# Key tiles of 128 keys, packed scatters, experts and combination moved forward, and expert pairs in a software pipeline behind the attention

## The chip, the cores and the metric

The kernel runs on one core of one Trainium2 chip. The metric is the device time of one execution in microseconds (us), of which lower is better; three executions of the kernel before are shown, and their median counts. Engines are named as in the profile: PE is TensorE's multiplication, PEld its weight load, DVE VectorE, ACT ScalarE, POOL GpSimd and SP SyncE, which only issues transfers.

## The reference

Eight images of 64 channels and 56 x 56 pixels pass through three stages, in float32:

```python
x = x + conv3x3(group_norm(x, 32 groups), weight)        # 64 -> 64 channels
t = tokens(x)                                            # 3136 tokens of 64 per image
t = t + softmax(q(ln(t)) k(ln(t))^T / 8) v(ln(t))        # one head of 64, each image by itself
n = ln(t)
logits = n @ gate_w + gate_b                             # 16 experts
top-2 of softmax(logits), renormalised -> dispatch
h = silu(n @ w1[e]) * (n @ w2[e])                        # hidden 128
t = t + sum_e dispatch[e] * (h @ w3[e])
```

## The kernel before, in words

An image's 3136 tokens are cut in 7 chunks of 448 tokens (CHUNK, CHUNKS), a chunk in 4 tiles of 112 (TILE, PER), an image so in 28 tiles (TILES). There are 56 chunks (ALL). The program is one list of **bodies**, written out in full, one for each chunk: body n = 7u + c attends with the 448 queries of chunk c of image u. Bodies -8 to -1 come ahead of the attention, bodies 0 to 55 attend, and bodies 56 to 77 come behind it. A body is a row of 28 slots, i = 0 to 27, and in each slot every engine's program has at most one step of each kind, in the same order on all. Nothing reorders them: an engine that waits holds back all of its later steps, of later bodies too.

Slot i of a body that attends, on PE: `scores` (L1047, L1049) multiplies key tile i with the body's queries, in two fp32r parts q_a and q_b, into one of two banks ps_s; ACT takes its exponential (L636) into one of 6 tiles prob; every fourth slot `weigh` (L1060) multiplies four such tiles with the values v_s into ps_o, in plain float32, the even tiles in the upper and the odd ones in the lower half of the array's columns. Between them stand the **maxima for the next body**: 28 products of a query tile with 448 keys (L1026), each reduced to its row maximum on DVE (L788), spread over slots 2 to 24 by `max_reach` (MAX_FROM, MAX_TO). They give the shift of the next body's exponentials (`shift`, L1034, slot 26).

STEPS lists the other work and its slot; LAG says how many bodies a stage runs behind (or ahead of) the attention. *pre* (7 bodies ahead): convolution, tokens, first layer norm, keys k_a and values v_s of the next image. *post* (1 behind): attended tokens into `kept`, second layer norm, gate, top 2; in the body of chunk 0, slots 14 to 26 also **route** the image that has just ended: counts, ranks and places (`slot`) of all its tokens among the experts. *scatter* (8 behind, one chunk a body): POOL copies each token's row twice into sorted_x in HBM, with 8 indirect transfers of 112 rows (L502). *experts* (15 behind): per chunk of sorted rows 5 **pairs** of 128-row tiles, 2 in the last chunk, 32 an image. A pair is four steps on PE, each followed by one on ACT or DVE: `fx` transposes, `hidden` multiplies with w1 and w2 (fp32r, two parts), ACT's tanh and DVE's two products, `turn` transposes, `down` multiplies with w3 and ACT copies into fy, which SP stores to sorted_y. *combine* (22 behind): POOL gathers with 8 indirect transfers (L515), waiting for the whole image's fy (L509) and for the combination before it (L510, the buffers got1, got2 and tc are single); DVE weighs and adds (L944 to L949) in slot 19, PE transposes, ACT copies, SP stores the output.

So the 22 bodies behind the attention are: 56 with the last post and route; 57 to 63 with the scatter of image 7; 56 to 70 with 66 pairs (EXPERT_STEPS_ALONE, four slots a pair); 56 to 77 with a combination each. POOL's order in a body is scatter, norm2, norm1, gather (`body`, L527). Ahead of the first image POOL sets constants (L442 to L477) and zeroes both sorted_x with 28 transfers (L483); its first step of the group norm (L535) is behind them.

## Time and profile before

| | us |
|---|---|
| three executions, median (lowest to highest) | 3304.51 (3299.92 to 3306.05) |
| the profiled execution: its own time | 3304.37 |
| its span | 3301.5 |
| ahead of the first score / bodies 0 to 55 / behind the last score | 198.8 / 2701.4 / 401.3 |

| engine | busy us | share of the span |
|---|---|---|
| PE | 2755.8 | 83% |
| DVE | 1950.5 | 59% |
| ACT | 1426.9 | 43% |
| POOL | 1004.9 | 30% |

The profiled execution is 0.14 us from the median, and 2.9 us of it lie outside of its span. Lines L1047 to L1085 are in PE's functions, L788 to L949 in DVE's, L553 to L636 in ACT's and L502 to L535 in POOL's. Matmul records give the time from a product's start to its end with the array's latency in it, so consecutive ones overlap; from one start to the next is what a product takes of PE.

### The profile page before, as it was taken

What the parts mean: (1) busy time and instruction counts of PE and PEld (TensorE: products, weight loads), DVE (VectorE), ACT (ScalarE), POOL (GpSimd) and SP (SyncE); (2) the same over time, 40 slices, a digit from 0 to 9 for tenths busy, and PEclk for the clock granted to TensorE, in tenths of its full rate; (3) what the DMA queues carried; (4) which work ended last, traced back from release to release, by engine and by line L of the source; (5) the groups of instructions that cost most, each with busy time, mean ns of one, the idle gap of its engine ahead of it and who ended that gap; (6) DMA issues with size and microseconds to landing.
All of it is one profiled execution on the core that took longest, in us unless ns stands there. A gap on an engine that the chain in (4) does not pass through costs nothing.

```text
span 3301.5 us, 47374 instructions
## 1 busy us (share of the span) xinstructions
PE 2755.8 (83%) x14345; PEld 1688.3 (51%) x14345; DVE 1950.5 (59%) x5316; ACT 1426.9 (43%) x3169; POOL 1004.9 (30%) x1084
## 2 busy tenths in 40 slices
PE   0489998998999999998999899998999898967760
PEld 0245554554555555555555455554555555545550
DVE  1366667667666666668566765667656656442221
ACT  0134444444555544554445454454544454523330
POOL 4000002221212134234242332423324323347444
PEclk9679999999999999999999999999999999965555
DMA  6200000111111111211112111111111111123321
GB/s 142 63 21 20 19 16 26 30 29 33 47 43 41 44 44 50 54 44 52 51 50 52 49 49 51 50 49 40 50 47 41 38 43 43 42 64 91 82 60 31
DMA packets 218415, 156.13 MB, mean 47 GB/s; under 512 B 94400, under 2 KB 208832, under 8 KB 218176
## 3 DMA queue, kind: packets, MB, share of 16 engines
q1 hardware_dynamic: 187008, 106.12, 12.2%
q0 software_dynamic: 31168, 46.98, 5.9%
q8 instruction: 131, 2.15, 0.3%
q14 instruction: 108, 0.88, 0.1%
HBM read 89.29 MB, written 63.70 MB: 46 GB/s over the span
## 4 chain that ended last, share of the span: by engine, by line
PE 58%; DVE 24%; issue 8%; POOL 6%; ACT 2%; DMA 2%; SPq 1%; POOLq 0%; DVEq 0%; ACTq 0%
PE ps_o L1060 17%; DVE max_part L788 9%; PE ps_s L1047 8%; PE ps_m L1026 8%; PE ps_s L1049 6%; PE ps_x L1202 5%; PE ps_z L1085 4%; POOL got L515 3%; PE ps_x L1217 2%; PE ps_z L1210 1%; POOL sorted_x L502 1%; PE ps_y L1136 1%; PE ps_y L1120 1%; DVE top_i L845 1%; DVE got L944 1%
## 5 line engine op out<-in xcount | busy, mean ns | idle before, releaser
L788 DVE TENSOR_REDUCE max_part<-ps_m 112x1 f32<-112x448 f32 x1568 | 947.9, 621 | 528.5 <-PE ps_m L1026 518.9
L636 ACT ACTIVATE prob<-ps_s 112x448 f32<-112x448 f32 x1568 | 848.9, 543 | 598.8 <-PE ps_s L1049 575.1
L1026 PE MATMUL ps_m<-k_a,q_a 128*112 128x448 f32 x1568 | 589.3, 394 | 140.4 <-DVE max_part L788 129.5
L1060 PE MATMUL ps_o<-prob,v_s 112*64 112x448 f32 x3136 | 695.9, 566 | 0.3 <-issue 0.3
L1047 PE MATMUL ps_s<-q_a,k_a 128*112 128x448 f32 x1568 | 661.9, 422 | 16.0 <-ACT prob L636 9.9
L1049 PE MATMUL ps_s<-q_b,k_a 128*112 128x448 f32 x1568 | 573.5, 366 | 0.0
L502 POOL DMA_INDIRECT sorted_x<-xn,slot x448 | 427.3, 954 | 283.7 <-issue 260.3
L515 POOL DMA_INDIRECT got<-sorted_y,slot x448 | 424.9, 948 | 213.8 <-issue 126.5
L1026 PEld LDWEIGHTS ps_m<-k_a,q_a 128*112 128x112 f32 x1568 | 276.4, 176 | 311.1 <-DVE max_part L788 273.1
L525 POOL TENSOR_TENSOR ln_s<-ln_s,minus_half 112x4 f32<-112x4 f32 x56 | 58.1, 1037 | 1175.7 <-DVE ln_s L706 1175.7
L1047 PEld LDWEIGHTS ps_s<-q_a,k_a 128*112 128x112 f32 x1568 | 276.2, 176 | 184.5 <-issue 123.4
L1060 PEld LDWEIGHTS ps_o<-prob,v_s 112*64 112x64 f32 x3136 | 193.9, 138 | 310.4 <-issue 283.7
L1049 PEld LDWEIGHTS ps_s<-q_b,k_a 128*112 128x112 f32 x1568 | 277.1, 177 | 12.9 <-issue 3.0
L932 DVE SCALAR_TENSOR_TENSOR up<-th,ps_x 128x256 f32<-128x256 f32 x256 | 107.3, 419 | 271.1 <-ACT th L604 270.9
L1202 PE MATMUL ps_x<-w_hi,fxT 128*128 x512 | 204.5, 402 | 15.1 <-ACT fxT L600 9.4
L521 POOL TENSOR_TENSOR ln_s<-ln_s,minus_half 112x4 f32<-112x4 f32 x56 | 56.4, 1007 | 445.9 <-DVE ln_s L706 445.9
L1085 PE MATMUL ps_z<-xg,wT 128*64 128x224 f32 x1344 | 153.4, 381 | 35.2 <-ACT xg L553 35.2
L609 ACT ACTIVATE hidT<-ps_z 128x256 f32<-128x256 f32 x190 | 73.1, 385 | 233.6 <-PE ps_z L1210 233.6
L604 ACT ACTIVATE th<-ps_x 128x256 f32<-128x256 f32 x256 | 98.5, 385 | 155.7 <-PE ps_x L1202 154.0
L1202 PEld LDWEIGHTS ps_x<-w_hi,fxT 128*128 128x128 f32 x512 | 107.7, 210 | 112.6 <-issue 88.2
L1202 PE MATMUL ps_x<-w_lo,fxT 128*128 x512 | 158.6, 313 | 0.0
L782 DVE TENSOR_TENSOR q_b<-ps_y,q_a 128x448 fp32r<-128x448 f32 x56 | 35.0, 625 | 208.9 <-ACT q_a L624 208.9
(170 smaller groups left out, 3004.0 us busy)
## 6 DMA issues: line engine op xcount, KB each, us to landing
fx<-sorted_x SPq DMA_DIRECT2D x48, 384.0 KB
sorted_y<-fy SPq DMA_DIRECT2D x48, 320.0 KB, 3.1
fx<-sorted_x SPq DMA_DIRECT2D x56, 256.0 KB
xh<-in_x SPq DMA_DIRECT2D x96, 126.0 KB, 2.7
x_st<-in_x SPq DMA_DIRECT2D x100, 112.0 KB, 2.6
sorted_x<-fy POOLq DMA_DIRECT2D x24, 320.0 KB
sorted_x<-xn,slot POOLq DMA_INDIRECT x448
got<-sorted_y,slot POOLq DMA_INDIRECT x448
```

Of the source, the lines that this page charges most:

```text
L502: g.indirect_dma_start(out=sorted_x[b % 2], out_offset=bass.IndirectOffsetOnAxis(ap=slot[:, b % 4, k, j:j + 1], axis=0), in_=xn2[:, j, :, ...
L515: g.indirect_dma_start(out=got[:, j, :], out_offset=None, in_=sorted_y[b % 2], in_offset=bass.IndirectOffsetOnAxis(ap=slot[:, b % 4, m, ti ...
L604: a.activation(th[:], ps_x[:].rearrange("p (t m h) -> p t m h", t=2, m=2)[:, :, 0, :], ACT.Tanh, scale=0.5).then_inc(s["th_ready"], 1)
L636: a.activation(prob[(at.n * TILES + i) % PROBS][:], ps_s[i % 2][0:TILE, 0:CHUNK], ACT.Exp).then_inc(s["p_ready"], 1)
L788: v.tensor_reduce(max_part[:, m % PER, m // PER:m // PER + 1], ps_m[m % 2][0:TILE, 0:CHUNK], AX.X, ALU.max).then_inc(s["max_red"], 1)
L932: v.scalar_tensor_tensor(out=up[:], in0=th[:], scalar=1.0, in1=both[:, :, 0, :], op0=ALU.add, op1=ALU.mult).then_inc(s["f_link"], 1)
L1026: t.matmul(ps_m[m % 2][0:TILE, 0:CHUNK], q_a[:, bass.ds(n % 2, 1), j * TILE:(j + 1) * TILE].rearrange("p a c -> p (a c)"), k_a[u % 2][:, k ...
L1047: t.matmul(ps_s[i % 2][0:TILE, 0:CHUNK], k_a[p][:, keys], q_a[:, now, :].rearrange("p a c -> p (a c)"), start=True, stop=False)
L1049: t.matmul(ps_s[i % 2][0:TILE, 0:CHUNK], k_a[p][:, keys], q_b[:, now, :].rearrange("p a c -> p (a c)"), start=False, stop=True).then_inc(s ...
L1060: t.matmul(ps_o[side:side + CHANNELS, 0:CHUNK], v_s[u % 2][:, i, :], prob[(n * TILES + i) % PROBS][:], start=(i < 2), stop=(i >= TILES - 2 ...
L1085: last = t.matmul(ps_z[64 * half:64 * half + 64, 0:CHUNK // 2], wT[:, down, k, :], xg[:, top:top + ROWS // 2, k:k + SIDE], start=(down == ...
L1202: last = t.matmul(ps_x[:, j * 2 * HIDDEN:(j + 1) * 2 * HIDDEN], fxT[:, j * SLOTS:(j + 1) * SLOTS], w12[part][:, bass.ds(picked[2 * pair + ...
```

## The change

1. **Key tiles of 128.** The image's 3136 keys become 25 tiles (KEY_TILES) of 128 places. Chunks 0 to 5 fill 112 places of tiles 0 to 23; of chunk 6, one tile of 112 tokens goes to tile 24, and the other three (GIVING) are cut in 21 pieces of 16 keys, which fill places 112 to 127 of tiles 0 to 20. Tiles 21 to 24 keep 16 empty places (key 0, value and its weight 0). A body has 25 slots instead of 28: 25 `scores`, exponentials of 128 rows and `weigh` products. The maxima stay 28 products of 448 keys, but the last 4 of a body, and every seventh body's queries, are now two products, of 112 and 336 keys, and all read keys in pieces. The values of the pieces go from v_give to v_s with 7 transfers an image on SP. The maxima are spread over slots 2 to 21. The group `weigh` of the last slots has 5 tiles, the others 4. The constants now also hold zeros for v_s and k_a.
2. **Packed scatter.** The image's 7 scatters run in the first three bodies behind it: chunk 0 in that of chunk 0, then three and three. Two semaphores by turns let a scatter start when the one before the last has landed.
3. **Experts and combination sooner.** Experts run 11 behind instead of 15, fy is double. Images 0 to 5 are combined two chunks a body, in the bodies of chunks 5, 6 and 0 (and one in that of chunk 1) from 19 bodies behind their first chunk on; images 6 and 7 one chunk a body, from body 61 (LATE) to 74, at slot 22. got and tc are double, and POOL issues the gather one body ahead.
4. **Pipeline of pairs.** Behind the attention a slot has `fx` of a pair, `hidden` of the pair before, `down` of the pair three before and `turn` of the one two before; `hidden` has two banks, those of ps_s. A body's store of fy is issued one body later, the last two together, behind the output of that body.

```diff
-LAG = {"pre": -CHUNKS, "post": 1, "scatter": 1 + CHUNKS, "experts": 1 + 2 * CHUNKS, "combine": 1 + 3 * CHUNKS}
+LAG = {"pre": -CHUNKS, "post": 1, "experts": CHUNKS + 4}
+SCATTERS = ((0,), (1, 2, 3), (4, 5, 6), (), (), (), ())
+COMBINES = {5: (0, 1), 6: (2, 3), 7: (4, 5), 8: (6,)}
+COMBINE_AT, COMBINED_AT = (10, 16, 22), (11, 18, 23)
+LATE = ALL + 5
+LAST = LATE + 2 * CHUNKS - 1
 EXPERT_STEPS = sorted(
-    (at + 5 * g, order, name, g) for g in range(PAIRS) for at, order, name in
+    (at + (0, 4, 8, 13, 17)[g], order, name, g) for g in range(PAIRS) for at, order, name in
...
-MAX_FROM, MAX_TO = 2, 25
+MAX_FROM, MAX_TO = 2, 22
-PROBS = 6
-SHIFT = 26
+PROBS = 7
+KEY_TILES = -(-TOKENS // 128)
...
+SHIFT = 23
+    def combines(self):
+        if self.n >= LATE:
+            return [(2, ALL - 2 * CHUNKS + self.n - LATE)] if self.n <= LAST else []
+        image, place = (self.u - 3, self.c + CHUNKS) if self.c < 2 else (self.u - 2, self.c)
+        chunks = COMBINES[place] if place in COMBINES and 0 <= image < BATCHES - 2 else ()
+        return [(slot + 2 - len(chunks), CHUNKS * image + c) for slot, c in enumerate(chunks)]
...
+def expert_steps(at):
...
+    steps, pairs = [], alone_pairs()
+    here = [k for k, (mine, _) in enumerate(pairs) if mine.n == at.n]
+    if here and here[-1] == len(pairs) - 1:
+        here += [len(pairs) + k for k in range(3)]
+    for place, k in enumerate(here):
+        for name, behind in (("fx", 0), ("hidden", 1), ("gated", 1), ("down", 3), ("turn", 2)):
+            if 0 <= k - behind < len(pairs):
+                steps.append((1 + 4 * place, name) + pairs[k - behind])
...
+        def keys_of(p, c):
+            k = key_tiles(p)
+            if c < CHUNKS - 1:
+                return [(0, CHUNK, k[:, c * PER:(c + 1) * PER, 0:TILE])]
+            own = OWN * TILE
+            return [(0, own, k[:, KEY_TILES - OWN:KEY_TILES, 0:TILE]), (own, CHUNK, k[:, 0:FILLED, TILE:128])]
...
+                for mine in at.stores():
...
+                    wait_apart(sp, s["fy_ready"], ONE + mine.pairs_before() + mine.pair_count())
...
             for p in range(2):
-                chain(g.memset(v_s[p][:, :, 0:1], 1.0))
+                chain(g.memset(v_s[p][96:128, :, :], 0.0))
+                chain(g.memset(v_s[p][0:TILE, :, 0:1], 1.0))
+                chain(g.memset(key_tiles(p)[:, FILLED:KEY_TILES, TILE:128].bitcast(f32), 0.0))
+            chain(g.memset(v_give[:, :, 0:1], 1.0))
...
+                early = at.scatters() if at.c else []
+                early = early[:1] if at.attends else early
+                for m in early:
+                    scatter(m)
...
+                for _, k in At(*divmod(at.n + 1, CHUNKS)).combines():
+                    gather(k)
+                for m in at.scatters()[len(early):]:
+                    scatter(m)
...
-                    t.matmul(ps_m[m % 2][0:TILE, 0:CHUNK],
-                             q_a[:, bass.ds(n % 2, 1), j * TILE:(j + 1) * TILE].rearrange("p a c -> p (a c)"),
-                             k_a[u % 2][:, kb * CHUNK:(kb + 1) * CHUNK], start=True, stop=True).then_inc(s["max_done"], 1)
+                    for first, last, keys in keys_of(u % 2, kb):
+                        done = t.matmul(ps_m[m % 2][0:TILE, first:last],
+                                        q_a[:, bass.ds(n % 2, 1), j * TILE:(j + 1) * TILE].rearrange("p a c -> p (a c)"),
+                                        keys, start=True, stop=True)
+                    done.then_inc(s["max_done"], 1)
```

## Rows read from the trace of the kernel before

**Rows 1.** The page: busy time by engine; TensorE's granted clock in 40 slices.
```profile
PE 2755.8 (83%) x14345; PEld 1688.3 (51%) x14345; DVE 1950.5 (59%) x5316; ACT 1426.9 (43%) x3169; POOL 1004.9 (30%) x1084
PEclk9679999999999999999999999999999999965555
```
**Rows 2.** Stages: stretch, length, busy us (instructions) by engine, clock, DMA share, GB/s.
```profile
198.80:2900.20 2701.40, 2474.46 (x13168) 1478.90 (x13169) 1774.36 (x4847) 1304.73 (x2852) 743.78 (x774) 0.99 0.16 41
2900.20:3301.50 401.30, 216.70 (x918) 173.35 (x916) 109.72 (x285) 106.75 (x292) 219.30 (x233) 0.54 0.27 67
```
**Rows 3.** The same view for bodies 3, 17, 25, 26, 28 and 52, in this order.
```profile
317.30:358.30 41.00, 38.25 (x197) 21.57 (x197) 27.48 (x75) 18.44 (x38) 2.01 (x2) 1.00 0.07 18
926.70:975.60 48.90, 45.98 (x259) 28.56 (x258) 31.36 (x85) 25.39 (x58) 9.64 (x10) 1.00 0.17 45
1327.30:1377.90 50.60, 46.64 (x262) 28.89 (x261) 32.73 (x89) 25.70 (x59) 17.23 (x18) 1.00 0.20 53
1377.90:1430.20 52.30, 48.24 (x261) 29.33 (x260) 32.72 (x89) 25.58 (x59) 17.31 (x18) 0.97 0.20 51
1481.70:1534.90 53.20, 45.91 (x230) 25.71 (x229) 42.29 (x113) 22.76 (x49) 21.92 (x23) 0.97 0.25 64
2713.30:2761.50 48.20, 43.36 (x231) 26.75 (x230) 29.05 (x78) 24.30 (x56) 16.19 (x17) 1.00 0.17 43
```
**Rows 4.** Timeline of PE in body 3: start us, length us, engine, line, operation.
```profile
344.92 0.36 PE L1026 MATMUL ps_m<-k_a,q_a 128*112 128x448 f32 x1
345.12 0.36 PE L1047 MATMUL ps_s<-q_a,k_a 128*112 128x448 f32 x1
...
345.83 1.72 PE L1060 MATMUL ps_o<-prob,v_s 112*64 112x448 f32 x8
347.48 0.45 PE L1047 MATMUL ps_s<-q_a,k_a 128*112 128x448 f32 x1
```
**Rows 5.** Timeline of PE's weight loads in the same stretch.
```profile
344.92 0.17 PEld L1047 LDWEIGHTS ps_s<-q_a,k_a 128*112 128x112 f32 x1
```
**Rows 6.** PE's longest wait in bodies 17, 25, 28 and 52: us, times, longest.
```profile
PE ps_m L1026 <- DVE max_part L788: 1.8, 2, 1.1
...
PE ps_m L1026 <- DVE max_part L788: 2.9, 3, 1.1
...
PE ps_m L1026 <- DVE max_part L788: 4.0, 3, 2.9
...
PE ps_m L1026 <- DVE max_part L788: 3.5, 4, 1.0
```
**Rows 7.** Timeline of PE: four value tiles in body 26.
```profile
1419.10 3.08 PE L1060 MATMUL ps_o<-prob,v_s 112*64 112x448 f32 x8
```
**Rows 8.** Timeline of POOL ahead of the first image.
```profile
17.93 0.64 POOL L476 MEMSET fy<- 128x640 f32 x1
...
72.73 0.58 POOL L535 TENSOR_TENSOR gn_rstd<-gn_var,minus_half 128x1 f32<-128x1 f32 x1 [1.75 <-DMA sorted_x<-fy]
```
**Rows 9.** Timeline of POOL behind the attention: scatters and gathers, idle time in brackets.
```profile
2931.35 1.07 POOL L502 DMA_INDIRECT sorted_x<-xn,slot  x1 [11.84 <-issue]
...
2941.47 0.95 POOL L515 DMA_INDIRECT got<-sorted_y,slot  x1 [0.30 <-issue]
...
3200.56 0.93 POOL L515 DMA_INDIRECT got<-sorted_y,slot  x1 [8.57 <-DMA sorted_y<-fy]
...
3209.21 0.94 POOL L515 DMA_INDIRECT got<-sorted_y,slot  x1 [0.30 <-issue]
```
**Rows 10.** Busy time in one body of five pairs behind the attention; columns as in rows 2.
```profile
3098.10:3116.20 18.10, 15.47 (x66) 12.92 (x65) 5.73 (x14) 7.68 (x21) 7.84 (x10) 0.50 0.34 82
```
**Rows 11.** Timeline of SP: the last store of fy.
```profile
3197.52 0.48 SPq L415 DMA_DIRECT2D sorted_y<-fy  x1
```
**Rows 12.** Timeline of all engines at the end.
```profile
3290.46 0.93 POOL L515 DMA_INDIRECT got<-sorted_y,slot  x1 [0.30 <-issue]
3292.84 0.76 DVE L944 TENSOR_TENSOR got<-got,gates 112x256 f32<-112x256 f32 x2 [11.87 <-DMA got<-sorted_y,slot]
```

More of the change, by code:

```diff
@@ L430, in _ @@
+            for n in range(-CHUNKS - 1, LAST + 1):
+                at, nxt = [At(*divmod(m, CHUNKS)) for m in (n, n + 1)]
+                body(at, (nxt.u + 1, nxt.c) if n >= -CHUNKS and nxt.u + 1 < BATCHES else None)
             sp.wait_ge(s["stored"], ONE + 16 * ALL)
@@ L499, in scatter @@
                     wait_apart(pool, s["fx_b_in"], ONE + (b - 1) * (CHUNKS - 1) * 16)
-                for j in range(at.chunk("scatter") * PER, (at.chunk("scatter") + 1) * PER):
+                for j in range(c * PER, (c + 1) * PER):
                     for k in range(TOP):
@@ L1239, in body @@
                 done = 0
-                for i in range(TILES):
+                experts = expert_steps(at)
+                for i in range(KEY_TILES):
                     if at.attends:
```

363 lines of the change are left out of this document (201 added, 162 removed).

## The prediction

> **What bounds the kernel now.** I read the page first, then the stages, then single bodies, then the timelines. PE is busy 83% of the span, and the clock row falls only ahead of the attention and behind it [rows 1]. The attention is 2701.4 us with PE busy 2474.5 of them; behind it lie 401.3 us in which PE is busy 216.7 and POOL 219.3 [rows 2]. The two stages have different limits.
>
> In the attention PE sets the pace. A light body (no experts) takes 41.0 us with PE busy 38.3; with five pairs 48.9 and 46.0; with a combination too 50.6 and 46.6 [rows 3]. So a pair costs (48.9 - 41.0) / 5 = 1.58 us and a combination 1.7. What PE does not fill is nearly all one wait, that of the maxima's bank for DVE: 1.8 us, 2.9 with a combination, 4.0 in a body that routes [rows 6]. DVE itself is busy only 31 to 33 us of these, 42 in the routing one [rows 3]: it is late at single moments, when layer norms or combinations stand ahead of a reduction, not as a whole.
>
> Behind the attention nothing is full for long; it is a row of serial stretches: 31.1 us of last post and route up to the first scatter (2900.2 to 2931.35), seven bodies in which POOL does 8 scatters and 8 gathers, the experts of image 7 at some 18.1 us a body [rows 10], and from 3200.56 the gathers of image 7, each waiting for the combination before it [rows 9].
>
> **Key tiles of 128.** Three slots go from each of 56 bodies. By starts, a score product takes 0.20 us (344.92 to 345.12 for its like), and four value tiles 1.65 (345.83 to 347.48), 0.41 each [rows 4]: 3 x (0.20 + 0.20 + 0.41) = 2.4 us at least. The first product behind other work starts the next 0.08 us later still, so I take 2.6, and 2.8 as the most. ACT loses three exponentials a body, and is not what anyone waits for.
>
> Added: the last four maxima are two products each, with one more weight load. No row has a product of 112 fp32r columns. Its bounds: in proportion the columns are the same and it costs nothing but a start, 0.05 us; or 112 columns take as long as the 448 of the nearest row, 0.20 to 0.25. I take 0.1, near the lower, since the work is the same in columns: 0.4 us a body, 0.2 to 1.0. That keys are read in pieces has no row; I take nothing, the same bounds covering it.
> In the rows the load of 0.17 us lies beside the product before it, as the 0.20 us from start to start leave no room for it [rows 4, 5]. The Trainium skill says otherwise ("TensorE: Matmul & The Clock Gate", Part 3, on the mechanism of tiling): a load overlaps products in flight only if it goes to other rows of the array. By that the four extra loads would stand bare, 0.7 us a body instead of 0.4, 17 us more in the sum. The trace disagrees with it for long products.
>
> That is 2.6 - 0.4 = 2.2 us of PE work less. How much of it becomes time? DVE's work does not shrink, and its 28 reductions now have to fit in slots 2 to 21. Body 52 shows it: it lacks the convolution and first norm, PE is busy 3.3 us less than in body 25, but the body is only 2.4 us shorter, and the wait for DVE 0.6 longer [rows 3, 6]. A quarter of what PE saves goes to the wait. So 2.2 x 0.75 = 1.65 us a body, 92 us in all. Ends: 2.8 - 0.2 with no loss, 146 us; 2.4 - 1.0 with half lost, 39 us.
>
> **Moved into the attention.** Experts 11 behind instead of 15: bodies 11 to 55 hold 207 pairs where bodies 15 to 55 held 190: 17 x 1.58 = +27 us. Combinations: 39 instead of 34, 5 x 1.7 = +9. The routing body had the light chunk of 2 pairs and one combination; now it has 5 pairs and two. DVE's 42.3 us there become 42.3 + 3 x 0.8 + 1.7 = 46.4 (four combining steps of 0.42 [rows 12], and (5.7 - 1.7) / 5, about 0.8, for a pair [rows 10]); its wait was already 4.0 against 2.9 elsewhere. For six such bodies I add 1.3 us each, +8 (0 to 15). POOL's scatters come two or three to a body, some 20 to 30 us of its 48; the norms' powers stand behind one scatter as before. SP gets the waits of two outputs; the next slice is loaded ahead of the second. The 7 transfers of v_give wait for slot 12 on SP, ahead of the load of the next slice, whose own wait is for a later or equal slot; nothing is late by them. Both at nothing; if the slice came late, a body would lose one pair's 1.6 us.
> Attention: -92 + 27 + 9 + 8 = **-48 us** (-110 to +12).
>
> **Ahead of it.** POOL's constants stand before the zeroing, and that before the group norm's power at 72.73, which waits for the last of these transfers [rows 8]. 640 columns take 0.64 us, so the two fills of 1600 take 3.2, and the four small ones about 0.6: **+4 us** (2 to 6).
>
> **Behind the attention.** Times from the last score.
> Post and route: 31 us, plus 3 more pairs' DVE work (2.4) and one more combination (1.7) in body 56, and 2 for waits: 37. 56 scatters without gathers between: 8 take 2931.35 to 2941.47, so 1.25 each [rows 9], 70 us: 107. Landing and the load of the slice, together 5 (1.5 for a gather from 3291.4 to 3292.84 [rows 12], and for the load as much as from the last store to the gather behind it, 3 [rows 9, 11]): image 7's experts start at 112. The 17 pairs of image 6 are hidden under the scatters.
> A pair takes p. Before, five pairs and one combination took 18.1 us, PE 15.5, ACT 7.7, DVE 5.7, all at half clock [rows 10]. The pipeline takes the latencies out: PE's own work then bounds p at (15.5 - 1.0) / 5 = 2.9 at 1.2 GHz, and 1.6, the attention's price, at 2.4 GHz; ACT's part is 1.5. Whether the clock rises no row tells: PE's gaps shrink, yet with a rise they would come back. I take the middle, 2.3.
> Body 60 has 5 pairs, and SP issues the store of image 6's last chunk only behind both loads of body 60, which follow its transposes: 112 + 11.5 = 123.5, plus 3 (store 3197.52 to gather 3200.56 [rows 9, 11]) = 126.5. POOL is idle for those 20 us. First combination at 126.5 + 9.9 + 4.6 (landing, DVE's four steps, transposes and copy) = 141. Each body then ends with a combination, which costs 2.9 on top of its pairs (18.1 = 5 x 3.0 + 2.9): 14.4 us a body, over gathers' 9.9, so the five bodies 62 to 66 end at 213. The last store stands behind that output: 216. Then 56 gathers without waits at 1.236 (3200.56 to 3209.21 for seven [rows 9]), 69, and from the last gather's end to the span's end 10 (3291.4 to 3301.5 [rows 12]): **295 us instead of 401, -106**. At p = 1.6: 274 (-127); at p = 2.9: 313 (-88).
>
> **The sum.** 3304.4 + 4 - 48 - 106 = 3154 us. The profiled run is 0.14 us off the median, so it needs no correction.
>
> **The rivals.**
> (a) *PE's saving is all time.* DVE's waits are of a burst, not a share: 1.0 to 1.1 us is the longest one whatever PE has to do. Then the tiles give 2.4 x 56 = 134, and the time is 3154 - 42 = 3112. Against it: body 52.
> (b) *DVE takes PE's place in the attention.* The reductions lose two slots and the bodies of chunks 5, 6 and 0 get two combinations, each of which lengthens the wait by 1.1 us [rows 6]. Then the tiles give nothing: 3304.4 + 4 + 44 - 106 = 3246. Against it: DVE is busy 65% of a body.
> (c) *The pipeline does not do what it says*: the clock stays at 1.2 GHz, PE is the bound behind the attention, 2.9 a pair: 3172.
> (d) *Slower than before*: the clock falls within the attention. Four value tiles took 3.08 us instead of 1.72 in body 26, behind a wait for DVE, and this body took 52.3 instead of 50.6 [rows 3, 4, 7]; one such fall costs 1.7 us. If each body's denser waits bring them, the loss grows by 1.7 a fall; it turns the sum from 3154 past 3304 at 90 falls, 1.6 a body. With three a body 3154 + 56 x 5.1 = 3440. For it: the waits for DVE grow just there. Against it: bodies of more waits, as 28, show one fall at most.
>
> **How the numbers follow.** The forecast, both gains with a part lost, 0.45; (a) 0.2; (b) 0.12; (c) 0.18; (d) 0.05. The range takes (a), (b) less its far end, (c), and the ends of the tail's p: 3080 to 3230. A measurement of this kernel can tell about 0.2% from no change. All cases but (d) are faster by far more: faster 0.94, same 0.01, slower 0.05.
>
> **What would show it.** Light bodies at 39 us and those with five pairs at 47.3; PE's wait for L788's successor at 2.5 to 4 us a body; a routing body of 57 to 59. Behind the attention: scatters back to back for 70 us, POOL idle 20 us, gathers of image 6 at a body's pace, those of image 7 back to back for 69; a period of 2.3 us a pair between tanhs, and the clock row. A first score later by 4 us. I am wrong if the wait for DVE exceeds 5 us a body, if the split products cost over 0.25 us each, if a wait of SP or POOL that I passed over holds the slices back, or if the clock falls in many bodies.

## The result, and the profile after

The changed kernel takes 3265.0 us in the median (3262.5 to 3266.0) against 3304.3 (3299.9 to 3306.1): 0.9878 of before, with an interval of 0.9867 to 0.989. The forecast was 3154, range 3080 to 3230. So the kernel is faster, as said, but by 39 us and not by 150, and the time lies outside the range.

The page of the changed kernel: PE's busy time, and the granted clock in 40 slices.
```profile
PE 2639.2 (81%) x13913; PEld 1706.6 (52%) x13913; DVE 1953.0 (60%) x5340; ACT 1316.9 (40%) x3009; POOL 1004.7 (31%) x1089
PEclk9679998999999999999899989999999999998785
```
Beside rows 1, PE is busy 117 us less, yet its share has fallen from 83% to 81%, and a few slices of the attention are no longer a 9. The stages of the changed kernel, attention and behind it (columns as in rows 2):
```profile
203.90:2969.00 2765.10, 2446.64 (x12954) 1570.44 (x12955) 1798.45 (x4922) 1232.81 (x2764) 791.85 (x830) 0.96 0.16 43
2969.00:3263.80 294.80, 127.08 (x696) 99.36 (x694) 87.74 (x231) 68.53 (x219) 167.33 (x177) 0.68 0.28 69
```
Ahead of the first score it takes 203.9 us instead of 198.8 (forecast 4 more, got 5). The attention takes 2765.1 instead of 2701.4: the forecast had 48 less, it is 64 more. Behind the last score it takes 294.8 instead of 401.3, where 295 was forecast. The whole miss, 111 us, lies in the attention. Its bodies 2 and 3 (light), 12 (five pairs), 26 (five pairs, two combinations) and 28 (the routing body):
```profile
279.90:321.60 41.70, 37.95 (x190) 22.00 (x190) 27.46 (x75) 16.61 (x36) 2.02 (x2) 0.96 0.07 18
320.00:360.10 40.10, 36.32 (x189) 21.66 (x189) 27.44 (x75) 16.57 (x35) 2.02 (x2) 1.00 0.07 19
713.50:763.20 49.70, 44.50 (x252) 29.33 (x251) 31.24 (x85) 23.47 (x55) 2.01 (x2) 1.00 0.13 35
1426.70:1480.80 54.10, 47.75 (x260) 31.85 (x259) 34.13 (x93) 24.48 (x57) 17.04 (x18) 0.94 0.20 49
1536.00:1598.30 62.30, 52.52 (x262) 35.22 (x260) 45.62 (x120) 25.44 (x58) 12.65 (x13) 0.86 0.16 41
```
Against rows 3, PE does 1.9 us less in light body 3 and 1.5 less with five pairs. Body 3 is only 0.9 shorter, and the one with five pairs is 0.8 longer. Body 2 has the same work as body 3, but the clock falls in it (0.96), and it takes 41.7 us where the light bodies of before take 41.0; bodies 4 and 9 are like it. In bodies 26 and 28 the clock is 0.94 and 0.86. PE's waits in body 12, and one more of body 26:
```profile
PE ps_x L1300 <- ACT fy L686: 2.3, 3, 0.8
PE ps_z L1285 <- ACT hidT L680: 1.7, 3, 0.6
PE ps_m L1119 <- DVE max_part L873: 0.9, 1, 0.9
...
PE ps_y L1243 <- DVE logit L922: 1.8, 1, 1.8
```
The first two are new: in the bodies of before the wait for the maxima was the longest [rows 6], 1.8 us in the one of five pairs, and no wait for ACT reached it. Both come from the offsets 0, 4, 8, 13, 17 of a body's pairs. A pair's turn is in its slot 5, and where the next pair starts 4 slots later that is the next pair's slot 1, its fx, and both write ps_z. Its down is in slot 7, the next pair's 3, its hidden, and both write ps_x. So PE writes a bank, and at once needs it empty. The timeline of PE in body 12:
```profile
726.88 0.44 PE L1308 MATMUL ps_z<-ident,hid 128*128 128x128 f32 x2
727.88 0.41 PE L1285 MATMUL ps_z<-ident,fx 128*128 128x128 f32 x2 [0.56 <-ACT hidT L680]
...
731.47 0.38 PE L1300 MATMUL ps_x<-w_hi,fxT 128*128 x1 [0.75 <-ACT fy L686]
```
Three such pairs of collisions a body make 4 us, where five pairs follow each other in 17 slots instead of 20.

**The ledger of the attention.** To compare kernels I split the attention of each one's profiled execution in three. The waits are the sum of PE's idle times before its products. The half clock is what the clock took: half of the time in which PE was busy at a granted clock of 0.5. The work is the rest: busy time less that half. The three add up to the attention by construction. The half is a rough price: spread 2 has the same products as the changed kernel and comes out with 27 us less work, so its half clock is put too high by about as much.

| kernel | attention | work | waits | half clock |
|---|---|---|---|---|
| before | 2701.4 | 2443.5 | 226.9 | 31.1 |
| changed (first run) | 2765.1 | 2354.3 | 318.5 | 92.4 |
| changed (third run) | 2765.6 | 2353.9 | 317.9 | 93.8 |
| changed, 28 tiles | 2716.2 | 2449.6 | 223.3 | 43.4 |
| early down | 2710.8 | 2349.9 | 314.0 | 47.2 |
| spread 2 | 2732.9 | 2327.5 | 277.4 | 128.1 |
| early down, later combinations | 2723.7 | 2357.5 | 327.2 | 39.3 |
| filler | 2745.4 | 2375.4 | 317.2 | 52.8 |
| one maximum | 2756.1 | 2346.4 | 325.9 | 83.9 |
| early down and filler | 2713.7 | 2363.8 | 304.4 | 45.9 |

From before to after: work 89 less, waits 92 more, half clock 61 more, in all 64 more.

**Behind the attention.** POOL's timeline in the changed kernel: the last scatter of image 7, the first gather behind the idle time, a gather of image 6's last bodies, the first of image 7 and the last of all.
```profile
3073.41 0.94 POOL L561 DMA_INDIRECT sorted_x<-xn,slot  x1 [0.30 <-issue]
3094.50 0.95 POOL L576 DMA_INDIRECT got<-sorted_y,slot  x1 [20.15 <-DMA sorted_y<-fy]
...
3168.23 0.93 POOL L576 DMA_INDIRECT got<-sorted_y,slot  x1 [5.35 <-DVE t_out L1035]
...
3183.91 1.05 POOL L576 DMA_INDIRECT got<-sorted_y,slot  x1 [6.04 <-DMA sorted_y<-fy]
...
3252.80 0.93 POOL L576 DMA_INDIRECT got<-sorted_y,slot  x1 [0.30 <-issue]
```
Nearly all of it stands where the sum had it; the numbers are compared point by point below.

### The profile page after: what moved, and what is told of

Its sections match the earlier page's. It is cut to its first block, busy times and chain, and to the rows that moved or that the text cites. A ratio compares the mean times of both kernels' runs of the same rounds, so it can differ in the third digit from the quotient of the medians.

```text
span 3263.8 us, 46526 instructions
## 1 busy us (share of the span) xinstructions
PE 2639.2 (81%) x13913; PEld 1706.6 (52%) x13913; DVE 1953.0 (60%) x5340; ACT 1316.9 (40%) x3009; POOL 1004.7 (31%) x1089
## 4 chain that ended last, share of the span: by engine, by line
PE 60%; DVE 18%; issue 9%; POOL 6%; ACT 5%; DMA 2%; SPq 1%; POOLq 0%; DVEq 0%; ACTq 0%
PE ps_o L1156 16%; PE ps_m L1119 9%; DVE max_part L873 7%; PE ps_s L1142 7%; PE ps_s L1144 6%; PE ps_x L1300 5%; PE ps_z L1182 3%; PE ps_z L1285 2%; POOL sorted_x L561 2%; PE ps_x L1315 2%; POOL got L576 2%; ACT hidT L680 1%; PE ps_z L1308 1%; ACT fy L686 1%; DVE up L1017 1%
## 5 line engine op out<-in xcount | busy, mean ns | idle before, releaser
L708 ACT ACTIVATE prob<-ps_s 128x448 f32<-128x448 f32 x1400 | 757.4, 543 | 731.9 <-PE ps_s L1144 719.4
L1119 PE MATMUL ps_m<-k_a,q_a 128*112 128x448 f32 (+2 forms) x1792 | 607.5, 383 | 87.0 <-DVE max_part L873 68.3
L1156 PE MATMUL ps_o<-prob,v_s 128*64 128x448 f32 x2800 | 642.6, 568 | 0.0
L1142 PE MATMUL ps_s<-q_a,k_a 128*128 128x448 f32 x1400 | 598.7, 428 | 4.9 <-ACT q_a L700 3.7
L1144 PE MATMUL ps_s<-q_b,k_a 128*128 128x448 f32 x1400 | 524.4, 375 | 0.0
L1142 PEld LDWEIGHTS ps_s<-q_a,k_a 128*128 128x128 f32 x1400 | 273.2, 195 | 115.4 <-issue 88.8
L1156 PEld LDWEIGHTS ps_o<-prob,v_s 128*64 128x64 f32 x2800 | 183.2, 140 | 286.8 <-issue 247.8
L1144 PEld LDWEIGHTS ps_s<-q_b,k_a 128*128 128x128 f32 x1400 | 274.5, 196 | 9.0 <-issue 2.6
L671 ACT ACTIVATE fxT<-ps_z 128x256 fp32r<-128x256 f32 x256 | 98.3, 384 | 276.9 <-PE ps_z L1285 174.2
L1285 PE MATMUL ps_z<-ident,fx 128*128 128x128 f32 x512 | 109.7, 297 | 121.6 <-ACT hidT L680 76.1
```

The source lines that it names most:

```text
L708: a.activation(prob[(at.n * KEY_TILES + i) % PROBS][:], ps_s[(at.n * KEY_TILES + i) % 2][:, 0:CHUNK], ACT.Exp).then_inc(s["p_ready"], 1)
L1119: done = t.matmul(ps_m[m % 2][0:TILE, first:last], q_a[:, bass.ds(n % 2, 1), j * TILE:(j + 1) * TILE].rearrange("p a c -> p (a c)"), keys, ...
L1142: t.matmul(ps_s[t_of % 2][:, 0:CHUNK], k_a[p][:, keys], q_a[:, now, :].rearrange("p a c -> p (a c)"), start=True, stop=False)
L1144: t.matmul(ps_s[t_of % 2][:, 0:CHUNK], k_a[p][:, keys], q_b[:, now, :].rearrange("p a c -> p (a c)"), start=False, stop=True).then_inc(s[" ...
L1156: t.matmul(ps_o[side:side + CHANNELS, 0:CHUNK], v_s[u % 2][:, i, :], prob[(n * KEY_TILES + i) % PROBS][:], start=(i < 2), stop=(i >= KEY_T ...
L1285: last = t.transpose(ps_z[:, j * SLOTS:(j + 1) * SLOTS], fx[:, 2 * pair + j, :, :].rearrange("p a b -> p (a b)"), ident[:])
```

## The experiments

Two theories of the miss in the attention were put against each other. **Theory one**: the key tiles save PE's work as forecast, and the schedule that came with them gives it back, by collisions and by falls of the clock that follow them; repair the schedule and some 90 us come back. **Theory two** (rival b): what PE saves turns into waits whatever the schedule is, because DVE and ACT have each their own chain through a body. What the clock takes was to be told apart from both. In the expectations theory one is A or just the theory, its part on the clock alone is F, and theory two is B.

**The change without its key tiles (tiles28_c).** It ran on one chip with the changed kernel unedited (same_third), filler_c and onemax_c.
```
-    (at + (0, 4, 8, 13, 17)[g], order, name, g) for g in range(PAIRS) ...
+    (at + 5 * g, order, name, g) for g in range(PAIRS) ...
-MAX_FROM, MAX_TO = 2, 22
+MAX_FROM, MAX_TO = 2, 25
-KEY_TILES = -(-TOKENS // 128)
+KEY_TILES = TILES
-SHIFT = 23
+SHIFT = 26
```
and with it the tiles of 112 keys in scores, exponentials and values, the unsplit maxima, no v_give and no zeroing of the tiles.

> The changed kernel unedited, as the base that the other kernels on this chip are held against. On a chip like the first, every theory: 3262 to 3266 us, 0.987 to 0.988 of before, with some 203 us of half clock inside the attention.

> Everything of the change but the key tiles: 28 tiles of 112 keys, maxima to slot 25, and the experts' offsets five slots apart as before. Theory (the tiles save PE some 120 us, and their offsets 0, 4, 8, 13, 17 give all of it back as collisions of a pair's turn and down with the next pair's fx and hidden, and as falls of the clock): PE's waits inside the attention some 230 us instead of 316, half clock some 70 instead of 203, attention 2735 to 2765, time 3235 to 3265, thus no slower than the changed kernel. Rival (the tiles are worth the 92 us net that was forecast, and something else of the change costs them): the changed kernel without its tiles is some 90 us slower, 3355.

Measured: the changed kernel 3264.5 us, 0.9875 (0.986 to 0.9891) of before; without its key tiles **3210.1**, 0.9709 (0.9696 to 0.9723). The key tiles, which should have brought 92 us in the attention, cost 54 in all, 49 of them there. The ledger says how: from 28 tiles to 25, work 96 less, waits 95 more, half clock 50 more. Ahead of the first score there are 5.6 us more (198.2 and 203.8), the zeroing of the tiles, and behind the last 2.9. One light body (3) and one of five pairs (25) of the kernel with 28 tiles, then the same two of the changed kernel:
```profile
317.90:359.20 41.30, 38.15 (x196) 21.58 (x196) 27.36 (x75) 18.32 (x38) 2.01 (x2) 1.00 0.07 18
1367.70:1416.80 49.10, 46.13 (x257) 28.59 (x257) 31.23 (x85) 25.20 (x57) 17.11 (x18) 1.00 0.13 33
```
```profile
319.90:360.00 40.10, 36.31 (x188) 21.65 (x188) 27.45 (x75) 16.60 (x35) 2.02 (x2) 1.00 0.07 19
1377.80:1427.40 49.60, 44.44 (x248) 29.21 (x248) 31.27 (x85) 23.21 (x54) 17.26 (x18) 1.00 0.13 33
```
DVE's time is the same in both. In the light body PE's 1.8 us less become 1.2 less of time, in the body of pairs 1.7 less become 0.5 more. And body 3 is a light body in which the clock holds. The eight light bodies 1 to 5 and 8 to 10 take 332.3 us together with 28 tiles and 332.1 with 25: what the tiles bring there goes to falls in bodies 2, 4, 8 and 9, where 28 tiles have one, in body 8, and to 2.7 us more of waits in body 8. So even where no pair can collide with another nothing is left. My expectation had the kernel with 28 tiles at 3235 to 3265. Its waits are as expected (223 us for 230) and its time at half clock is longer (94 for 70), so what came out smaller is its work.

**Down a slot sooner (early_down).** No down shares a slot with the next hidden any more, but a turn still shares one with the next fx twice a body (slots 15 and 19) instead of three times. It ran on a second chip, with the changed kernel unedited again (same_again) and the two of the next experiment.
```
-    (at + (0, 4, 8, 13, 17)[g], order, name, g) for g in range(PAIRS) for at, order, name in
-    ((1, 1, "fx"), (3, 3, "hidden"), (3, 4, "gated"), (5, 0, "turn"), (7, 2, "down")))
+    (at + (0, 5, 10, 14, 18)[g], order, name, g) for g in range(PAIRS) for at, order, name in
+    ((1, 1, "fx"), (3, 3, "hidden"), (3, 4, "gated"), (5, 0, "turn"), (6, 2, "down")))
```


> The changed kernel once more, unedited, so that the runs beside it have it on their own chip. Ratio to the kernel before 0.988 if the chip is like the first; on a chip like that of the four runs before, where the kernel before takes 3932, all theories leave it open whether it lies with spread (1.005) or onemax (0.991).

> A pair's down stands one slot sooner, and pairs begin in slots 1, 6, 11, 15 and 19, in bodies that attend. No down shares a slot with a hidden any more; two turns share one with an fx instead of three. Theory A (the shared slots are what PE waits in): the waits of hidden for fy (96.6 us) go and those of fx for hidT fall from 76 to about 50; the wait for the maxima's bank rises from 84 towards 137. Net some 70 us of waits, and fewer falls of the clock: ratio to same_again 0.96 to 0.98. Theory B (maxima and DVE are the bound): 0.995 to 1.0, the wait for the maxima taking all of it.

Measured: unedited 3262.4, 0.9872 (0.9855 to 0.9888); early_down **3212.9**, 0.9706 (0.9684 to 0.9727). To the unedited kernel that is 0.985, between the ranges of the two theories (0.96 to 0.98, and 0.995 to 1.0). The waits did not go the way theory one had it. PE's waits are the same in sum, 314.0 us against 315.5 on that chip; only their names have changed. Its body 25:
```profile
1369.90:1419.50 49.60, 43.99 (x249) 28.57 (x249) 31.14 (x85) 23.76 (x54) 17.02 (x18) 1.00 0.13 33
```
and what PE waits for in it:
```profile
PE ps_m L1119 <- DVE max_part L873: 2.3, 3, 1.3
PE ps_y L1228 <- DVE xn L915: 1.3, 1, 1.3
PE ps_z L1308 <- DVE hid L1021: 0.6, 1, 0.6
PE ps_z L1285 <- ACT hidT L680: 0.6, 1, 0.6
```
49.6 us as with the collisions, and 0.5 more than with 28 tiles, though PE has 2.1 less to do. Take a wait for ACT away, and PE is sooner at the next wait for DVE. Nearly the whole gain over the changed kernel, 52 us in the attention, is the clock: half clock 47.2 instead of 93. And beside the kernel with 28 tiles, whose half clock is 43, it is level: 3212.9 and 3210.1, 0.9706 and 0.9709 of before. So with two of six collisions a body left, the key tiles are still worth nothing.

How far is that theory two? Early_down has 91 us more waits than 28 tiles. Of these 50 end with DVE (243 against 193), as theory two says. The other 42 stand ahead of the fx (L1285), two a body, where turns still share a slot with them; the trace names ACT's copy for 22 of them and nothing for 20. These are the schedule's.

**Other places (spread2, early_later).**
```
-    (at + (0, 4, 8, 13, 17)[g], ...          (spread2)
+    (at + (0, 5, 8, 13, 16)[g], ...
```
```
-COMBINE_AT, COMBINED_AT = (10, 16, 22), (11, 18, 23)          (early_later, on top of early_down)
+COMBINE_AT, COMBINED_AT = (12, 16, 22), (13, 18, 23)
```


> Pairs begin in slots 1, 6, 9, 14 and 17: no step of a pair shares a slot with another pair's, nor an fx with the convolution. Two pairs overlap, so that a down follows the next pair's hidden by one slot and waits for DVE's product, some 0.8 us, twice a body. Theory A: the 173 us of shared-slot waits become some 70, ratio to same_again 0.96 to 0.98, near early_down. Theory B: 0.995 to 1.0.

> early_down and the first of two combinations in slot 12 instead of 10. Theory A2 (DVE combines ahead of the logits, PE waits 1.8 us for them in 16 bodies): 28 us less than early_down, with the falls of the clock of these bodies up to 45 less: ratio to early_down 0.985 to 0.992. Rival (the combining is what costs, wherever it stands): 0.997 to 1.0.

Measured: spread2 3224.4 (0.9739, 0.9716 to 0.9762), early_later 3228.6 (0.9772, 0.9755 to 0.9788). In spread2 no step of a pair shares a slot with another pair's. It has the fewest waits of the kernels with 25 tiles (277), but the most half clock, 128, or some 100 with the 27 us that the ledger seems to have put there from its work. Its longest wait is new: a down stands one slot behind the next pair's hidden, and both write ps_x.
```profile
PE ps_x L1315 <- DVE hid L1021: 101.4, 70, 3.0
```
So spread2 is no schedule without waits on a shared bank either. In nearly every body of five pairs its clock falls, and such a body takes 50 us or more. Body 53, five pairs without a convolution, has no fall: 46.5 us, where 28 tiles take 46.6. Bodies of two pairs do gain: the five from 17 to 45 take 42.2 to 42.8 us in early_down, against 43.1 to 43.6 with 28 tiles. (The profiled execution of spread2 took 3235.0 us, the slowest of four from 3210.5 on.) Early_later moves the combination behind the logits, and the wait for logit goes; one for t_out and more for the maxima stand in its place, 13 us more in all, and 8 more of work, against 8 less of half clock. It takes 1.005 of early_down, where 0.985 to 0.992 was expected: to move a single wait gained nothing.

No kernel here has 25 tiles and pairs that never wait on each other's banks. What is shown is that three schedules of pairs (the changed one, early_down, spread2) leave the key tiles worth nothing or less. That every schedule must is not shown.

**The clock (filler_c).** Why does it fall? The timeline of PE in body 28 of the changed kernel, on the chip of same_third:
```profile
1559.44 0.41 PE L1285 MATMUL ps_z<-ident,fx 128*128 128x128 f32 x2 [0.56 <-ACT hidT L680]
...
1563.64 0.98 PE L1243 MATMUL ps_y<-ident,t_out 112*128 112x112 f32 x4 [1.78 <-DVE logit L922]
1564.42 0.98 PE L1315 MATMUL ps_x<-w3s,hidT 128*128 x4
1566.15 0.57 PE L1300 MATMUL ps_x<-w_hi,fxT 128*128 x1 [0.75 <-ACT fy L686]
```
and two stretches of it, up to the fall of the granted clock and from it:
```profile
1559.00:1563.30 4.30, 2.42 (x16) 1.99 (x16) 3.75 (x9) 1.77 (x4) 1.01 (x1) 1.00 0.32 91
1563.30:1570.10 6.80, 5.71 (x21) 4.58 (x23) 3.96 (x22) 2.29 (x6) 5.02 (x6) 0.50 0.13 34
```
PE has idled 1.9 of 4.3 us, at the end of which the clock goes to 0.5, and for 6.8 us PE works at half speed. The wait for logit comes from the moved combinations (at slot 10 DVE has them ahead of the logits, slot 11 needs both); the kernel with 28 tiles has it too, 30.8 us in all. The experiment fills a part of it with products that nobody reads:
```
+                for _ in range(4 if i == 11 and len(at.combines()) == 2 else 0):
+                    t.matmul(ps_s[t_of % 2][:, 0:CHUNK], k_a[p][:, keys], q_a[:, now, :].rearrange("p a c -> p (a c)"),
+                             start=True, stop=True)
                 t.matmul(ps_s[t_of % 2][:, 0:CHUNK], k_a[p][:, keys], ...
```


> Four score products of no use (their result is overwritten) ahead of slot 11's in the sixteen bodies with two combinations, where PE waits 1.76 us for DVE's logits just ahead of a fall of the clock. Theory (the clock falls where PE has just paused twice): the products take the place of part of that pause, and the falls of these bodies go: half clock 203 down to 120 to 150 us, time 3225 to 3245. Rival one (the falls come from elsewhere): half clock still about 200, and the products lie in a wait that was there anyway, 3262 to 3268. Rival two (the products cost their own time and nothing else changes): 16 times 0.9 us, 3277.

Measured: 3247.7, 0.9838 (0.9824 to 0.9852), so 17 us less by adding 68 products; the bodies with two combinations that attend are seventeen. The expected gain was 20 to 40 us. The same body:
```profile
1550.44 0.41 PE L1288 MATMUL ps_z<-ident,fx 128*128 128x128 f32 x2 [0.56 <-ACT hidT L680]
...
1552.01 1.05 PE L1143 MATMUL ps_s<-q_a,k_a 128*128 128x448 f32 x4
...
1554.73 0.57 PE L1246 MATMUL ps_y<-ident,t_out 112*128 112x112 f32 x4 [1.05 <-DVE logit L922]
```
```profile
1550.10:1554.40 4.30, 3.23 (x20) 2.73 (x20) 3.75 (x9) 1.67 (x4) 1.01 (x1) 1.00 0.31 91
1554.40:1561.20 6.80, 4.89 (x27) 3.09 (x27) 4.90 (x25) 2.27 (x6) 5.13 (x6) 1.00 0.16 34
```
PE idles 1.1 us instead of 1.9, and the clock stays. The time at 0.5 in the attention falls from 206 to 111 us, and in the twenty bodies of chunks 5, 6 and 0 from body 12 on, among which are the seventeen of two combinations, from 147 to 65. In the ledger: half clock 41 less, work 21 more, waits 1 less. The wait for logit by itself is not enough for a fall. In early_down it is still 1.58 us in body 28, with no wait for ACT around it, and the clock stays at 1.00 from 1540.0 to 1551.1 (later in that body it falls). In these three stretches it is waits close together that cost the clock. For the falls elsewhere, those of the light bodies among them, no experiment shows the cause.

**Both at once (early_filled).** The edits of early_down and of the filler in one kernel.

> The changed kernel with a pair's down one slot sooner (offsets 0, 5, 10, 14, 18) and four score products of no use ahead of slot 11's in the bodies of two combinations. Alone the first gave 3212.9 us with 96 us of half clock left inside the attention, the second 3247.7 with 111 instead of 206. Theory (both act on the same falls of the clock, and few are left): half clock 50 to 80 us, the products' own time against it, 3200 to 3212. Rival one (they act on different falls and add up): half clock about 20, 3195. Rival two (the products only cost time here): 3225.

It ran on a third chip with plain, without the unedited kernel, so it is compared by the ratio to before. Measured: 3213.8, 0.9719 (0.9705 to 0.9733), the same as early_down. Half clock 45.9 instead of 47.2: both had removed the same falls, and what is left does not hang on this pause. It is 2 us outside the range expected; the products cost 14 us of work and gave 10 of waits back.

**The split of the last maxima (onemax_c).** The last chunk's maxima are taken over the last 448 key places in one product, so some keys' maxima are left out.
```
-                    for first, last, keys in keys_of(u % 2, kb):
+                    for first, last, keys in keys_of(u % 2, kb) if kb < CHUNKS - 1 else \
+                            [(0, CHUNK, k_a[u % 2][:, KEY_TILES * 128 - CHUNK:KEY_TILES * 128])]:
```


> The last chunk's maxima as one product over the last 448 key places instead of two over the keys that are there (so some keys' maxima are left out and added zeros' taken in). Four products and four weight loads fewer in each of 56 bodies. Theory (a further product costs some 0.1 us): 22 us less than the changed kernel, 3241 to 3245. Rival one (a product of 112 columns takes as long as one of 448, 0.25 us): 56 us less, 3209. Rival two (they lie in waits that are there anyway): 3262 to 3266.

Measured: 3260.4, 0.9865 (0.985 to 0.988), 4 us less than the changed kernel on that chip. The 224 products and loads are 7.5 us of work, 0.03 each, and their absence brings 8 us of waits, and 10 less of half clock. The 4 us are within the intervals of the two. The split is as good as free. This is rival two of the expectation, nearly: work that goes into waits which are there anyway.

**The pipeline behind the attention (plain).** The changed kernel with a body's pairs in their old order there.
```
-        for name, behind in (("fx", 0), ("hidden", 1), ("gated", 1), ("down", 3), ("turn", 2)):
-            if 0 <= k - behind < len(pairs):
-                steps.append((1 + 4 * place, name) + pairs[k - behind])
+    steps = sorted(((a + 4 * g, o, name, g) for g in range(len(mine)) for a, o, name in
+                    ((0, 0, "fx"), (3, 0, "hidden"), (3, 1, "gated"), (5, 0, "turn"), (8, 1, "down"))))
```


> The changed kernel with the pairs behind the attention in their old order, each pair's chain from fx to down inside its own body; everything else as changed. Theory (the pipeline takes latencies out of the five bodies of image 7's experts): they take 18.1 us each as before instead of 14.7, so 17 us, and the last post and the scatters' stretch some 3 more: 3282 to 3288. Rival (the bodies are paced by something else, the combination and the gathers): at most 5 us, 3264 to 3270.

Measured: 3287.2, 0.9944 (0.993 to 0.9957), so the pipeline brings 23 us by the ratios (0.9872 to 0.9878 for the unedited kernel), and the time lies at the upper end of what was expected. The attention is the same (2765.0). The stretch from 3108.0 to the end of the pairs in the kernel with the old order, then in the changed kernel:
```profile
3108.00:3201.00 93.00, 70.79 (x314) 57.89 (x314) 29.52 (x73) 36.85 (x102) 42.69 (x47) 0.59 0.29 72
```
```profile
3108.00:3181.50 73.50, 54.14 (x308) 44.61 (x308) 27.07 (x67) 30.95 (x100) 42.02 (x45) 0.83 0.39 92
```
Nearly the same products; the clock is granted at 0.83 instead of 0.59, and PE is busy 17 us less. Of the 19.5 us between the two stretches these are nearly all, and only 3 are idle time. But the idle time lies elsewhere. PE's waits inside the pairs (for hid, fxT and hidT) fall from 16.6 to 2.5 us, and the one wait a body for the combination's sum grows from 5.6 to 15.8. So the pipeline put many short gaps together into one a body, the clock is full in between, and the gain is the clock's.

**On two slower chips.** On two other chips the kernel before takes 3932.3 and 3931.5 us, 19% more than on the others. Four kernels ran on the first: spread (offsets 0, 3, 8, 11, 16), later (the combinations' slots as in early_later, nothing else), onemax and tiles28 (as above). Filler ran on the second, with later, onemax and tiles28 once more.

> Only the five pairs' slots in a body that attends change: first slots 1, 4, 9, 12, 17 instead of 1, 5, 9, 14, 18, so that no step of one pair shares a slot with a step of another. Theory A (a pair's down and turn stand in the slot of the next pair's hidden and fx, and PE waits there for ACT to empty the bank: 96.6 + 76.1 us of waits in the changed kernel): these waits go, the wait for the maxima's bank comes back to some 130 us from 84, and with fewer pauses the clock falls less often; attention 2765 -> about 2650, time 3265 -> about 3150 (3110 to 3190). Theory B (the denser maxima and DVE are the bound, the bank waits only stand where DVE's would): under 25 us less, 3240 to 3265. Theory C (the clock falls by itself in the denser attention): falls stay near 39 windows and the gain is under 100 us.

> The first of two combinations in a body stands in slot 12 instead of 10, its transposes in 13 instead of 11. Theory A2 (in slot 10 DVE combines ahead of the gate's logits, and PE's transposes wait for these: 28.3 us of waits in 16 bodies): 28 us of waits go, and as the bodies with two combinations are those whose clock falls twice or more, some 10 falls of 1.7 us with them: 3265 -> about 3220 (3205 to 3240). Rival (DVE's combining itself, 1.7 us, is what lengthens the body wherever it stands): within 10 us of 3265.

> The last four maxima of a body are one product of 448 keys again, over the last 448 places of the keys; this leaves out the maxima over 336 of the last chunk's keys and takes some twice, which changes only the shift of the exponentials. My forecast had 0.1 us for each split, 0.4 a body: 3265 -> 3243. If a second product costs as much as a long one (0.20 to 0.25): 3265 -> 3215. If starts hide it altogether: 3265.

> Everything of the change but the key tiles: 28 tiles of 112 keys and 28 slots, no pieces, whole maxima, spread over slots 2 to 24, pairs five slots apart. Theory A: no pair's steps meet, so attention is that of before plus the moved work, 2701 + 27 + 9, plus the double combinations' waits and falls, some 40: 2777; with 294 behind and 199 ahead 3270, that is the tiles bring nothing as long as the pairs meet. Theory B (dense maxima are the bound): the same number here, but then the run with spread pairs gains nothing. If the tiles are worth what I forecast (92 us) even so, 3355.

> The changed kernel with work added: in slot 11 of the 19 bodies with two combinations (18 of them attend and have five pairs) PE makes the slot's first score product four times more, 0.8 us, into the bank that it then overwrites. Behind it stands the 1.8 us wait for the logits, which takes the added work in. Theory F (the attention lost to pauses twice: once their own length, once by TensorE's clock, which falls behind two pauses close together and then costs about half of each low stretch; 203 us of low clock against 69 before): with one pause filled the clock stays up in most of these bodies, low stretches 203 -> about 110, and the kernel is faster by 30 to 50 us with more work: ratio 0.973 to 0.979 against the changed kernel's 0.987. Rival (only waits count, the clock falls by chance): 0 to 15 us slower, 0.987 to 0.992.

Measured, against before on the same chip: spread 1.0054 (1.0034 to 1.0073), later 1.0116 (1.0076 to 1.0156) and 1.0111 (1.0065 to 1.0157), onemax 0.9908 (0.9877 to 0.994) and 0.9888 (0.9843 to 0.9934), tiles28 0.9898 (0.9858 to 0.9938) and 0.987 (0.9829 to 0.9911), filler 0.997 (0.9948 to 0.9992). Beside 0.9709 for tiles28 and 0.9838 for the filler on an undisturbed chip, these say little on the theories: onemax and tiles28, 50 us apart there, are level here. Spread and later were not run elsewhere, so their verdict is open; early_later speaks against the second. A stretch of the filler kernel on the slow chip shows what is different:
```profile
960.24 0.93 POOL L561 DMA_INDIRECT sorted_x<-xn,slot  x1 [0.30 <-issue]
...
964.68 0.38 ACT L680 ACTIVATE hidT<-ps_z 128x256 f32<-128x256 f32 x1 [11.65 <-remote]
...
965.16 0.66 PE L1288 MATMUL ps_z<-ident,fx 128*128 128x128 f32 x2 [8.12 <-issue]
...
970.99 0.62 DVE L873 TENSOR_REDUCE max_part<-ps_m 112x1 f32<-112x448 f32 x1 [14.67 <-issue]
```
PE, ACT and DVE all stand for 8 to 15 us with nothing of the program to wait for, while POOL's indirect transfers go on at their pace. In the attention of this run PE stands 45 times for over 4 us, 355 us in all; in filler_c, the same kernel on the other chip, never. What holds the three is not in the trace, and stays open.

## Why the prediction was wrong, and where it was right

**Key tiles, PE's work: right in kind, too large.** 2.2 us a body were forecast (2.6 less 0.4 for the split). Measured 1.7 (96 / 56): the split costs 0.13 a body (7.5 / 56) and not 0.4, the three slots bring 1.8 and not 2.6. That is 27 us of the miss, and not the step that failed.

**Key tiles, "a quarter of what PE saves goes to the wait": wrong, and the step that failed.** It rested on one pair of bodies, 25 and 52, which differ in PE's work by a convolution and a norm that take work from DVE and ACT as well. In a light body 0.6 of PE's 1.8 us go to waits, a third. In a body with pairs all of it goes and more: waits are 2.2 us longer in body 25 of the changed kernel for 1.7 of work saved. Over the attention the waits grew by 95 us where the work fell by 96. My account of it is that DVE and ACT, though not full (31.4 and 25.4 us in the body of five pairs [rows 3]), hold the ends of three chains (maxima, norms, experts) that come round in every few slots, and that fewer slots for the same chains bring them closer together. For it speaks that in early_down PE's waits for DVE are 50 us longer than with 28 tiles while DVE's own time is the same; a part is the bank that steps of two pairs share, and no kernel without such sharing was tried. Rival (b), that DVE takes PE's place, at 0.12, comes nearest, but in the changed kernel itself it is ACT that PE waits for most (179 us, against 119 for DVE). Its price was 3246, and less the 29 us that the moved work was overcharged that is 3217. Early_down took 3213, which is close in part by luck, as its clock falls more and its bank waits stand in no rival.

**The schedule of the pairs: put at nothing without a reason.** The steps are in the diff: turn in slot 5 and fx in slot 1 are one slot when pairs are 4 apart, and so are down in 7 and hidden in 3, both on the same bank. It takes 4 us a body from PE. But the experiment shows that these waits stand for others: with 1.1 of the 4 us left, body 25 takes the same 49.6 us. What they do cost is the next point.

**Rival (d), the clock falls within the attention: its mechanism came, at 0.05, though not its size.** The forecast itself had no term for it. The half clock costs 92 us instead of 31, 61 more: 48 in the 41 bodies from body 15 on and 13 in the 15 ahead, 1.1 us a body and not the 5.1 of three falls. So it ate the gain without making the kernel slower than before. The prediction had the very case (3.08 us for four tiles in body 26 [rows 7]), but I took the count of falls from the bodies of before, where it was one at most. Of these 61 us, 50 came with the key tiles. And they do not come with the waits for the maxima, as I had it: these fell from 127 us in the attention to 66. The filler took 41 us of half clock away by shortening the wait for logit, and early_down 46 by moving the collisions, with the sum of waits the same.

**Moved into the attention: right in sign, too large.** The change without its tiles has an attention of 2716.2 us, 15 more than before, where 44 were forecast (27 + 9 + 8). Of this 12 are half clock, work is 6 more and waits 4 less. Why 17 pairs and five combinations more add so little to the ledger's work is open but for a part: a body of five pairs has a work of 46.0 in both kernels, a combination raises it to 46.6 in the kernel before, two raise it to 46.2 only in body 26 of the one with 28 tiles. The routing body did become longer by 6.9 us (60.1 against 53.2) with 28 tiles, near the forecast (three pairs 4.7, a combination 1.7 and 1.3 for waits, 7.7), and by 9 with the change: its wait for DVE's logits and the falls behind it.

**Ahead of the attention: right.** 4 forecast, 5.1 measured; 5.6 between 28 and 25 tiles, so it is the filling of the tiles (kernels with the same beginning differ here by up to 3 us, 201.7 to 205.0).

**Behind it: right nearly term by term, with some luck.** From the last score, forecast in brackets: first scatter at 35.7 (37), last scatter's end at 105.4 (107), first gather at 125.5 (126.5) after 20.15 us of idle (20), first combination's output at 140.8 (141), the first gather of image 7 at 214.9 (216), 56 gathers in 69.8 (69), the end at 294.8 (295). Between the first combination and the gather of image 7 errors cancel: four bodies take 14.8 us each (14.4), the fifth only 9.5, as its chunk has two pairs and not five, and the gather comes 5.4 us behind its output (3). Pairs follow each other by 2.2 us on average (2.3), at a clock of 0.83. So rival (c), a pipeline that doesn't raise the clock, is out. The middle between p of 1.6 and 2.9 was a guess, and that it came so close is luck. The rest worked because each stretch was a single chain with its own row before.

**The signs that I named.** The light body is 40.1 us, or 41.7 with a fall (39 forecast), five pairs 49.6 (47.3), the routing body 62 (57 to 59). PE's wait for the maxima is 0.9 in a body of pairs where 2.5 to 4 was to be: I looked for the wait for DVE to exceed 5 us, and what stood in its place was waits for ACT. "If the clock falls in many bodies" is the sign that did show.

**The sum, mended.** 3304.4 + 5 (ahead) + 15 (moved work) - 96 (tiles, work) + 95 (its waits) + 50 (its half clock) - 106.5 (behind) = 3267, against 3265. The version to keep is the change without its key tiles, 3210.1 us, or early_down with them, 3212.9: both beat both kernels, and the 3 us between them are no difference.

## What to carry to other kernels

Work taken from the busiest engine becomes time only where the others have what it needs next ready sooner too. Before a saving is counted, ask how many chains (write a bank, copy it, reduce it, use it) run through the shortened body, and whether the engines at their other ends now have fewer slots for the same steps. Here DVE was busy 63% and ACT 47% of a body of five pairs, and nothing of PE's 96 us was left. Where steps are put closer together, write down slot by slot which bank each one writes: two steps on one bank in one slot are a wait as long as the copy between them. And where PE is busy for 90% of a stage, its waits have to be read where they stand, since here a few close together took the clock too, and the falls cost 92 us beside 318 of waits.

## What the runs showed of the hardware

- The granted clock falls within a stage in which PE is busy 88% of the time. Ahead of the fall of body 28 PE had idled 1.9 of 4.3 us; with four products in one of these pauses it had idled 1.1, and the clock stayed. 68 products without use made the kernel 17 us faster.
- A load of 128 columns is hidden under the product before it here: loads of 0.18 to 0.20 us beside products that start 0.20 us apart, and the 224 further products with their loads of the split maxima cost 0.03 us each. What the Trainium skill states ("TensorE: Matmul & The Clock Gate", Part 3), that only loads to other rows overlap, would have made them 0.17 us each, and the trace disagrees with it also where products are short. The same Part also has loads to a background weight buffer pulled ahead of products in flight; the trace agrees with that.
- Two of the chips run the same kernels in 1.19 to 1.21 times the time, in part by stretches in which PE, ACT and DVE stand still together for 8 to 15 us while POOL's transfers go on; a comparison made there (onemax against tiles28: level) is not the one made elsewhere (50 us apart).
